# Sparse feed-forward: inner columns ordered by place in the quad, h turned one tile later, masks and masked product on POOL

## The chip, the cores and the metric

The kernel runs on one core of a Trainium2 chip. The metric is the device time of one launch in microseconds, the median of three runs. Lower is better.

## What is computed

A stack of six layers works on 1024 tokens of width 256, held as float32: a mixture of experts, attention, the mixture of experts again, a sparse feed-forward, a state-space layer, and the sparse feed-forward again with the same weights. The change touches only the two sparse feed-forward layers:

```python
def _sparsify_2to4(h):
    B, S, I = h.shape
    g = h.reshape(B, S, I // 4, 4)
    a = jnp.abs(g)
    _, idx = jax.lax.top_k(a, 2)
    pos = jnp.arange(4)
    mask = (pos == idx[..., 0:1]) | (pos == idx[..., 1:2])
    return (g * mask.astype(g.dtype)).reshape(B, S, I)
...
h = silu(x @ w_gate) * (x @ w_up)          # x: normalized tokens, 256 wide; h: 1024 wide
x = x + 0.5 * (_sparsify_2to4(h) @ w_down)
```

Of every four neighbouring inner columns (a quad) the two of largest magnitude stay, the others become zero; of equal magnitudes the earlier one stays.

## The kernel before

Each layer is a block in which the five engines run their own instruction streams in program order and meet at semaphores. `sparse_ffn_layer` walks over 8 token tiles of 128 tokens. In the profile's names its tiles carry the prefix `ffn_`; the same code runs twice, `ffn0` before the state-space layer and `ffn1` at the end of the kernel.

Products that need full precision are done in three passes (`matmul3`, lines 58 to 64): each float32 operand is split into a rounded high part and the remainder, both of type fp32r, and hi·hi, hi·lo and lo·hi are summed in PSUM. ACT makes a high part by a cast, DVE or POOL the low part by a subtraction.

For a tile t the steps are:

- `normalize` (DVE, L1226) makes xn; `turn_x` (PE, L1371) transposes it; `x_high` (ACT, L1330) and `x_low` (DVE, L1231) split it.
- `ups` (PE) computes gate and up for one half c of the inner columns, 12 matmuls of 512 columns for each half; `silu` (ACT, L1349) and `product` (DVE, L1239) turn them into half c of h.
- `mag` (ACT, L1359) takes magnitudes of the whole h. `sparsify` (DVE) compares them (`ffn_c`, L1252 to L1255), adds the comparisons to `wins` and `losses` (L1258 to L1260) and to a `score` per place (L1262 to L1265), and at the end (L1269, four operations) multiplies each place of h in place by its mask, score against a bound.
- `turn_h` (PE, L1397) transposes h in 8 pieces, `turned_high` (ACT, L1337) and `turned_low` (DVE, L1244) split it, `down` (PE) does 24 matmuls of 256 columns and `add` (DVE, L1274) adds half of the result to the residual.

The inner columns lie in memory as in the model, so that the four members of a quad are neighbours and one place of all 256 quads is read with a step of four float32 values (16 bytes).

Nothing but the order written in each engine's `body` and the semaphores sets the order of the work. In the body of tile t PE does ups(t, 0), the gate of ups(t, 1), turn_h(t−1), the up of ups(t, 1), turn_x(t+1), down(t−1). DVE does product(t, 0), turned_low(t−1), product(t, 1), x_low(t+1), sparsify(t), add(t−1), normalize(t+2). ACT does silu(t, 0), turned_high(t−1), silu(t, 1), x_high(t+1), mag(t). Tiles 3 to 6 run in a hardware loop of two tiles. POOL only makes the low parts of gate and down weights (L1199) at the start of the layer; there the weights are loaded in five transfers (L1206), the first of which holds the first half of the gate columns.

Of the kernel before, what the change touches and what calls it, by code (L numbers as in the profile page):

```python
# [1127 lines left out]
def sparse_ffn_layer(nc, xres, stats, ident, w_gate, w_up, w_down, tag, is_last=False):  # L1128
# [3 lines left out]
    with ExitStack() as ctx:  # L1132
# [24 lines left out]
        score = sp.sb("score", [P, 4, QUAD], BF16)  # L1157
        hT_hi = sp.sb("hT_hi", [P, KF, P], F32R)
# [16 lines left out]
        h_turned, hT_hi_done, hT_lo_done = (sp.sem(n) for n in ("h_turned", "hT_hi_done", "hT_lo_done"))  # L1175
        out_done, added = sp.sem("out_done"), sp.sem("added")
        ctx.callback(sp.clear_sems)
        block = ctx.enter_context(nc.Block())

        def tiles(eng, body):  # L1180

            for t in range(3):
                body(t, t % 2)
            with eng.Fori(1, TT // 2 - 1) as i:
                for b in (1, 0):
                    body(2 * i + 2 - b, b)
            body(TT - 1, 1)

        def static(t):
            return isinstance(t, int)  # L1190

        def part(n, c):
            return slice(0, D) if n == "down" else slice(c * BANK, (c + 1) * BANK)

        def split_low(eng, ops, n, c):

            eng.wait_ge(w_hi_done, w_parts.index((n, c)) + 1)
            cols = part(n, c)
            ops.tensor_tensor(w_lo[n][:, :, cols], w_raw[n][:, :, cols], f32(w_hi[n][:, :, cols]),  # L1199
                              ALU.subtract).then_inc(w_lo_done[n], 1)  # L1200

        @block.sync
        def _(sync):
            for n, c in w_parts:
                src = w_src[n].rearrange("(k p) n -> p k n", p=P)
                sync.dma_start(w_raw[n][:, :, part(n, c)], src[:, :, part(n, c)]).then_inc(loaded[n, c], 16)  # L1206

        @block.gpsimd
        def _(pool):
            for n, c in w_parts:  # L1210
                if n != "up":
                    split_low(pool, nc.gpsimd, n, c)

        @block.vector
        def _(dve):
# [1229 lines left out]
```

## Time and profile before

| | us |
|---|---|
| median of 3 runs (1861.74 to 1868.43) | 1865.56 |
| the profiled execution | 1868.16 |
| its span | 1866.3 |
| PE busy | 1601.7 (86% of the span) |
| DVE busy | 1146.5 (61%) |
| ACT busy | 863.0 (46%) |
| POOL busy | 442.4 (24%) |

The two sparse feed-forward layers stand at 892 to 1011 us (`ffn0`) and 1738 to 1860 us (`ffn1`) of the span. The other 1625 us are the layers that the change leaves alone. In the forty slices of the page the granted TensorE clock (PEclk) is 0.9 to 0.6 of full speed around the two ends of each of these layers.

### The profile page before, as it was taken

The numbers are of one execution on the slowest core, as the hardware profiler recorded it, in microseconds if no ns is written. First come the engines' busy times: TensorE is split into PE (matmuls) and PEld (weight loads), VectorE is DVE, ScalarE is ACT, GpSimd is POOL, SyncE is SP. The second block draws the span as 40 slices with busy tenths as digits, with TensorE's granted clock in tenths as the row PEclk, the third lists the DMA queues.
The fourth block names the chain that finished last, engine by engine and source line by source line (L and its number), as shares of the span: only waits on it lengthen the run. The fifth ranks groups of instructions, "written<-read, shape, count | busy, mean of one in ns | idle before, by whom it ended". The sixth has DMA issues, their size and how long they took to land. (4 is left out here: it accounts for less than half of the span.)

```text
span 1866.3 us, 25258 instructions
## 1 busy us (share of the span) xinstructions
PE 1601.7 (86%) x8136; PEld 1143.5 (61%) x8136; DVE 1146.5 (61%) x2073; ACT 863.0 (46%) x1270; POOL 442.4 (24%) x358
## 2 busy tenths in 40 slices
PE   3998399999999994998586877899998999998686
PEld 3665344444444443665475765787887888877575
DVE  4121688887878844221696765666766766764686
ACT  1222326655656662221332766566656655663321
POOL 1344400000000001343100112534534344433100
PEclk9999669999999996999797998999999999998888
DMA  8322100000000007422201000100101000100200
GB/s 302 95 46 37 43 21 12 10 4 12 12 12 11 0 1 273 92 46 38 87 1 29 21 8 19 29 18 23 29 12 29 23 17 23 29 12 12 68 0 23
DMA packets 70343, 73.78 MB, mean 40 GB/s; under 512 B 8480, under 2 KB 56992, under 8 KB 70240
## 3 DMA queue, kind: packets, MB, share of 16 engines
q1 hardware_dynamic: 60864, 58.35, 10.3%
q0 software_dynamic: 9376, 14.16, 4.3%
q8 instruction: 51, 0.84, 0.2%
q14 instruction: 52, 0.43, 0.1%
HBM read 56.50 MB, written 11.80 MB: 37 GB/s over the span
## 5 line engine op out<-in xcount | busy, mean ns | idle before, releaser
L784 DVE TENSOR_REDUCE attn_max_halves<-attn_scores 128x1 f32<-128x512 f32 x470 | 302.5, 686 | 70.4 <-PE attn_scores L1008 63.7
L913 ACT ACTIVATE attn_probs<-attn_scoresT 128x1024 f32<-128x1024 f32 x256 | 253.3, 1025 | 172.3 <-PE attn_scoresT L1021 171.8
L1008 PE MATMUL attn_scores<-attn_k_picks,attn_qT_pass 128*128 128x512 f32 x470 | 197.7, 452 | 5.6 <-DVE attn_max_halves L784 3.4
L1008 PEld LDWEIGHTS attn_scores<-attn_k_picks,attn_qT_pass 128*128 128x128 f32 x470 | 81.9, 188 | 152.6 <-DVE attn_max_halves L784 146.3
L1021 PE MATMUL attn_scoresT<-attn_qT_pass,attn_k_picks 128*128 128x512 f32 x512 | 169.0, 405 | 1.0 <-DVE attn_max_halves L784 1.0
L1447 DVE SCALAR_TENSOR_TENSOR ssm_scan_x<-ssm_scan_proj,ssm_w_conv,ssm_scan_x 128x1023 f32<-128x1023 f32 (+2 forms) x96 | 122.9, 1280 | 61.2 <-ACT ssm_scan_x L1442 58.2
L401 DVE TENSOR_TENSOR moe_h<-moe_silu,moe_up 128x512 f32<-128x512 f32 x46 | 31.6, 687 | 189.5 <-PE moe_up L516 189.5
L1035 PE MATMUL attn_o<-attn_probs,attn_v_group 128*32 128x512 f32 x1024 | 137.2, 608 | 0.6 <-ACT attn_probs L913 0.6
L2275 PE MATMUL ssm_scan_out<-ssm_scan_w_out,ssm_scan_v 128*128 128x256 f32 x464 | 118.2, 404 | 2.7 <-issue 2.7
L448 ACT ACTIVATE moe_silu<-moe_gate 128x512 f32<-128x512 f32 x46 | 27.5, 598 | 200.4 <-PE moe_gate L516 200.4
L62 PE MATMUL ssm_scan_proj<-ssm_xnT_hi,ssm_w_in_hi 128*128 128x512 f32 x256 | 115.1, 450 | 5.4 <-POOL ssm_scan_mask L1925 5.1
L286 POOL DMA_INDIRECT moe_sums<-moe_y,moe_token x46 | 73.0, 1588 | 165.2 <-DVE moe_y L410 159.2
L2142 ACT ACTIVATE ssm_scan_decay<-ssm_scan_cum,ssm_neg_cum 128x128 f32<-128x128 f32 x256 | 73.3, 368 | 79.0 <-PE ssm_scan_cum L2212 79.0
L1021 PEld LDWEIGHTS attn_scoresT<-attn_qT_pass,attn_k_picks 128*128 128x128 f32 x512 | 94.1, 189 | 22.3 <-ACT attn_probs L913 4.4
L63 PE MATMUL ssm_scan_proj<-ssm_xnT_lo,ssm_w_in_hi 128*128 128x512 f32 x256 | 105.9, 414 | 0.0
L64 PE MATMUL ssm_scan_proj<-ssm_xnT_hi,ssm_w_in_lo 128*128 128x512 f32 x256 | 105.6, 413 | 0.0
L2275 PEld LDWEIGHTS ssm_scan_out<-ssm_scan_w_out,ssm_scan_v 128*128 128x128 f32 x464 | 94.5, 205 | 17.5 <-issue 2.9
L1929 POOL TENSOR_TENSOR ssm_w_in_lo<-ssm_w_in,ssm_w_in_hi 128x512 fp32r<-128x512 f32 x31 | 42.2, 1362 | 239.8 <-ACT ssm_w_in_hi L2106 239.8
L516 PE MATMUL moe_gate<-moe_w_gate_up,moe_xT 128*128 x184 | 90.3, 614 | 1.3 <-ACT moe_xT L442 1.3
L2031 DVE SCALAR_TENSOR_TENSOR ssm_scan_x<-ssm_scan_x,ssm_d_skip,ssm_scan_y 128x1024 f32<-128x1024 f32 x32 | 41.0, 1281 | 80.9 <-PE ssm_scan_y L2253 80.9
L546 PE MATMUL moe_out<-moe_w_down,moe_hT 128*128 x368 | 87.1, 380 | 1.5 <-ACT moe_hT L454 1.5
L546 PEld LDWEIGHTS moe_out<-moe_w_down,moe_hT 128*128 128x128 f32 x368 | 69.8, 190 | 30.2 <-issue 23.0
(339 smaller groups left out, 3422.6 us busy)
## 6 DMA issues: line engine op xcount, KB each, us to landing
moe_w_gate_up<-in_moe_w SPq DMA_DIRECT2D x16, 512.0 KB, 11.2
moe_w_up<-in_moe_w SPq DMA_DIRECT2D x16, 512.0 KB, 11.1
moe_w_down<-in_moe_w SPq DMA_DIRECT2D x16, 512.0 KB, 11.0
ssm_w_in<-in_in_w SPq DMA_DIRECT2D x64, 128.0 KB, 2.2
attn_k_picks<-attn_kT SPq DMA_DIRECT2D x32, 128.0 KB, 2.4
ssm_scan_w_out<-in_out_w SPq DMA_DIRECT2D x8, 512.0 KB, 3.9
moe_sums<-main_residual SPq DMA_DIRECT2D x2, 1024.0 KB, 5.7
moe_rows<-moe_xn POOLq DMA_DIRECT2D x2, 1024.0 KB, 10.0
```

The source lines that it names most:

```text
L62: nc.tensor.matmul(out, lhs_hi, rhs_hi, start=start, stop=False)
L63: nc.tensor.matmul(out, lhs_hi, rhs_lo, start=False, stop=False)
L64: return nc.tensor.matmul(out, lhs_lo, rhs_hi, start=False, stop=stop)
L516: last = nc.tensor.matmul(bank[:].unsqueeze(1), xT[i % 2][:, k, :], w_in[name][:, bass.ds(e * KD + k, 1), :], start=(k == 0), stop=(k == K ...
L546: last = nc.tensor.matmul(out_ps[i % 2][:, 0:D].unsqueeze(1), hT[i % 2][:, k, :], w_dn[:, bass.ds(e * KI + k, 1), :], start=(k == 0), stop ...
L784: return nc.vector.tensor_reduce(rmax2[:, t, j, c:c + 1], chunk_bank(g, n), AX_X, ALU.max).then_inc(reduced, 1)
L913: nc.scalar.activation(probs[s % 2][:, 2 * pair:2 * pair + 2, :], st_ps[pair][:], ACT.Exp, scale=SCALE).then_inc(exp_done, 1)
L1008: nc.tensor.matmul(chunk_bank(g, n), qm[b][:, t * P:(t + 1) * P], kz[b][:, j, c * BANK:(c + 1) * BANK], start=True, stop=True).then_inc(sc ...
L1021: last = nc.tensor.matmul(st_ps[pair][:, j % 2, :], kz[b][:, j, kt * P:(kt + 1) * P], qe[b][:, half * BANK:(half + 1) * BANK], start=True, ...
L1035: last = nc.tensor.matmul(o_ps[j * STACK:(j + 1) * STACK, :], vg[b][:, kt, :], probs[s % 2][:, j, :], start=(kt == 0), stop=(kt == KT_TILE ...
L1447: return nc.vector.scalar_tensor_tensor(out[:, shift:], ps[:, :S - shift], w(k), out[:, shift:], ALU.mult, ALU.add)
L2275: last = nc.tensor.matmul(out[:, m, :], v[:, v_row(b * NORM_HEADS + jn), cols], w_out[:, jn, :], start=(jn == 0), stop=(jn == NORM_HEADS - 1))
```

## The change

The four places of a quad get blocks of their own: gate and up weights are reordered when they are split, so that h and its magnitudes are laid out as [place, quad] with 256 contiguous values for each place. The rows of the down weights are loaded in the matching order by four transfers. The four masks and the product of h with them move from DVE to POOL. PE, ACT and DVE run one tile further apart: `turn_h(t-1)` comes at the end of tile t, `down(t-2)` in the middle of it, and DVE does `sparsify(t-1)` at the start of tile t. The hardware loop is gone; the eight tiles are written out. The gate and up weights are loaded by rows (two transfers each) rather than by halves of the columns.

```diff
+        mask = sp.sb("mask", [P, 4, QUAD])
...
             eng.wait_ge(w_hi_done, w_parts.index((n, c)) + 1)
-            ops.tensor_tensor(w_lo[n][:, :, cols], w_raw[n][:, :, cols], f32(w_hi[n][:, :, cols]),
-                              ALU.subtract).then_inc(w_lo_done[n], 1)
+            for k in range(KD):
+                last = ops.tensor_tensor(in_places(w_lo[n], c)[:, k], by_place(w_raw[n], c)[:, k],
+                                         f32(in_places(w_hi[n], c)[:, k]), ALU.subtract)
+            last.then_inc(w_lo_done[n], 1)
...
+            for n in ("gate", "up"):
+                for k in range(KD):
+                    sync.dma_start(w_raw[n][:, k, :], src[n][k * P:(k + 1) * P, :]).then_inc(loaded[n, k], 16)
...
+            for t in range(TT):                                   # POOL
+                pool.wait_ge(scored, t + 1)
+                if t:
+                    pool.wait_ge(sparse, t)
+                for w, (op, bound) in enumerate(((ALU.is_ge, 2.0), (ALU.is_ge, 1.0), (ALU.is_le, 0.0), (ALU.is_le, 1.0))):
+                    last = nc.gpsimd.tensor_scalar(mask[:, w], score[:, w], bound, None, op)
+                last.then_inc(masked, 1)
+                pool.wait_ge(masked, t + 1)
+                nc.gpsimd.tensor_tensor(h[t % 2][:], h[t % 2][:], mask[:], ALU.mult).then_inc(sparse, 1)
...
-            def body(t, b):                                       # DVE
-                product(t, b, 0)
-                if not first:
-                    turned_low(t - 1)
-                product(t, b, 1)
-                if not last:
-                    x_low(t + 1, 1 - b)
-                sparsify(t, b)
-                if not first:
-                    add(t - 1)
+            for t in range(TT):
+                if t:
+                    sparsify(t - 1)
+                product(t, 0)
+                if t < LAST:
+                    x_low(t + 1)
+                if t >= 2:
+                    turned_low(t - 2)
+                    add(t - 2)
+                if t + 2 < TT:
+                    normalize(t + 2)
+                product(t, 1)
+            sparsify(LAST)
+            turned_low(LAST - 1)
+            add(LAST - 1)
+            if not is_last:
+                dve.wait_ge(added, LAST)
+                token_stats(nc, stats, xres, range(LAST))
+            turned_low(LAST)
+            add(LAST)
...
+            x_high(0)                                             # ACT
+            for n, c in w_parts:
+                split(n, c)
+            for t in range(TT):
+                silu(t, 0)
+                if t == 0:
+                    act.wait_ge(down_loaded, 64)
+                    nc.scalar.copy(w_dn_hi[:], w_dn[:]).then_inc(w_dn_hi_done, 1)
+                if t < LAST:
+                    x_high(t + 1)
+                silu(t, 1)
...
+                nc.scalar.activation(mag[:], h[t % 2][:], ACT.Abs).then_inc(mag_done, 1)
+                if t:
+                    turned(t - 1)
...
+            for t in range(TT):                                   # PE
+                ups(t, 0)
+                if t < LAST:
+                    turn_x(t + 1)
+                if t >= 2:
+                    down(t - 2)
+                ups(t, 1)
+                if t:
+                    turn_h(t - 1)
+            down(LAST - 1)
+            turn_h(LAST)
+            down(LAST)
```

`down` waits for the low parts of h in two halves of four pieces each, where it waited for both before its first matmul.

This is DVE's stream in one tile of the steady part before, from the last score of a tile to the last product of the next (`ffn_h<-ffn_silu,ffn_up` is `product`, `ffn_hT_lo` `turned_low`, `main_residual` `add`, `ffn_xT_lo` `x_low`):

```order
L1265 TENSOR_TENSOR ffn_score<-ffn_losses,ffn_c_23 128x256
L1269 SCALAR_TENSOR_TENSOR ffn_h<-ffn_score,ffn_h 128x256 x4
L1274 SCALAR_TENSOR_TENSOR main_residual<-ffn_out,main_residual 128x256
L1226 TENSOR_SCALAR ffn_xn<-main_residual,ffn_mean_var,ffn_rstd 128x256
L1239 TENSOR_TENSOR ffn_h<-ffn_silu,ffn_up 128x512
L1244 TENSOR_TENSOR ffn_hT_lo<-ffn_hT,ffn_hT_hi 128x512 x2
L1239 TENSOR_TENSOR ffn_h<-ffn_silu,ffn_up 128x512
L1231 TENSOR_TENSOR ffn_xT_lo<-ffn_xT,ffn_xT_hi 128x256
L1252 TENSOR_TENSOR ffn_c_13<-ffn_magnitude 128x512
```

And this is the same stretch of DVE's stream in the changed kernel:

```order
L1274 TENSOR_TENSOR ffn_score<-ffn_losses,ffn_c_23 128x256
L1252 TENSOR_TENSOR ffn_h<-ffn_silu,ffn_up 128x512
L1244 TENSOR_TENSOR ffn_xT_lo<-ffn_xT,ffn_xT_hi 128x256
L1279 TENSOR_TENSOR ffn_hT_lo<-ffn_hT,ffn_hT_hi 128x512 x2
L1284 SCALAR_TENSOR_TENSOR main_residual<-ffn_out,main_residual 128x256
L1239 TENSOR_SCALAR ffn_xn<-main_residual,ffn_mean_var,ffn_rstd 128x256
L1252 TENSOR_TENSOR ffn_h<-ffn_silu,ffn_up 128x512
L1259 TENSOR_TENSOR ffn_c_13<-ffn_magnitude 128x512
```

The four operations on h are gone, and `add` and `normalize` have moved between the two products of a tile.

On PE, before, the transposes of h stand inside the second half of `ups`, and `down` (`ffn_out`) follows at its end:

```order
L64 MATMUL ffn_gate<-ffn_w_gate_hi,ffn_xT_lo 128x512
L1397 MATMUL ffn_hT<-main_ident,ffn_h 128x128 x8
L62 MATMUL ffn_up<-ffn_w_up_hi,ffn_xT_hi 128x512
L63 MATMUL ffn_up<-ffn_w_up_lo,ffn_xT_hi 128x512
L64 MATMUL ffn_up<-ffn_w_up_hi,ffn_xT_lo 128x512
L62 MATMUL ffn_up<-ffn_w_up_hi,ffn_xT_hi 128x512
L63 MATMUL ffn_up<-ffn_w_up_lo,ffn_xT_hi 128x512
L64 MATMUL ffn_up<-ffn_w_up_hi,ffn_xT_lo 128x512
L1371 MATMUL ffn_xT<-main_ident,ffn_xn 128x128 x2
L62 MATMUL ffn_out<-ffn_w_down_hi,ffn_hT_hi 128x256
```

In the changed kernel `down` stands between the first half of `ups` (above it) and the second (below it), and the transposes of h close the tile:

```order
L64 MATMUL ffn_up<-ffn_w_up_hi,ffn_xT_lo 128x512
L1372 MATMUL ffn_xT<-main_ident,ffn_xn 128x128 x2
L62 MATMUL ffn_out<-ffn_w_down_hi,ffn_hT_hi 128x256
...
L64 MATMUL ffn_out<-ffn_w_down_hi,ffn_hT_lo 128x256
L62 MATMUL ffn_gate<-ffn_w_gate_hi,ffn_xT_hi 128x512
...
L64 MATMUL ffn_up<-ffn_w_up_hi,ffn_xT_lo 128x512
L1398 MATMUL ffn_hT<-main_ident,ffn_h 128x128 x8
```

So a `down` now stands ahead of the second half of gate and up in PE's queue, where it stood behind it.

## Rows read from the trace of the kernel before

**Rows 1.** Windows: stretch, length, busy time of each engine, granted clock, DMA

```profile
909.66:993.22 83.56, 68.70 (x381) 57.31 (x380) 73.79 (x152) 25.36 (x42) 1.33 (x1) 0.96 0.00 0
993.22:1010.87 17.65, 9.94 (x56) 9.13 (x56) 12.14 (x28) 2.23 (x3) 0.00 (x0) 0.71 0.00 0
1754.50:1842.46 87.96, 71.59 (x381) 60.11 (x380) 74.78 (x152) 25.54 (x42) 2.82 (x1) 0.92 0.00 1
1842.46:1860.42 17.96, 10.23 (x56) 9.42 (x56) 9.86 (x21) 2.23 (x3) 0.00 (x0) 0.71 0.00 1
```

**Rows 2.** Timeline of DVE in one tile of ffn1: start, duration, engine, line

```profile
1829.58 1.29 DVE L1244 TENSOR_TENSOR ffn_hT_lo<-ffn_hT,ffn_hT_hi 128x512 fp32r<-128x512 f32 x2
1830.85 0.69 DVE L1239 TENSOR_TENSOR ffn_h<-ffn_silu,ffn_up 128x512 f32<-128x512 f32 x1
1831.46 0.42 DVE L1231 TENSOR_TENSOR ffn_xT_lo<-ffn_xT,ffn_xT_hi 128x256 fp32r<-128x256 f32 x1
1832.67 1.10 DVE L1252 TENSOR_TENSOR ffn_c<-ffn_magnitude 128x512 bf16<-128x512 f32 x1 [0.79 <-ACT ffn_magnitude L1359]
...
1835.84 0.42 DVE L1258 TENSOR_TENSOR ffn_wins<-ffn_c,ffn_c 128x512 bf16<-128x512 bf16 x1
...
1837.63 2.19 DVE L1269 SCALAR_TENSOR_TENSOR ffn_h<-ffn_score,ffn_h 128x256 f32<-128x256 bf16 x4
```

**Rows 3.** Timeline of PE in the same tile

```profile
1830.92 0.39 PE L62 MATMUL ffn_out<-ffn_w_down_hi,ffn_hT_hi 128*128 128x256 f32 x1
...
1833.90 0.40 PE L62 MATMUL ffn_gate<-ffn_w_gate_hi,ffn_xT_hi 128*128 128x512 f32 x1
...
1836.65 0.39 PE L62 MATMUL ffn_gate<-ffn_w_gate_hi,ffn_xT_hi 128*128 128x512 f32 x1
...
1839.87 1.09 PE L1397 MATMUL ffn_hT<-main_ident,ffn_h 128*128 128x128 f32 x8 [1.70 <-DVE ffn_h L1269]
...
1841.96 0.40 PE L64 MATMUL ffn_up<-ffn_w_up_hi,ffn_xT_lo 128*128 128x512 f32 x1
```

**Rows 4.** Timeline in attention: a DVE sum of two SBUF operands, POOL idle, then busy

```profile
213.62 0.49 DVE L779 TENSOR_TENSOR attn_roped<-attn_qk_cos,attn_qk_sin 128x320 f32<-128x320 f32 x1
...
214.93 0.73 POOL L737 TENSOR_TENSOR attn_q_stack<-attn_roped,attn_q_stack 128x256 f32<-128x256 f32 x1
215.01 0.99 DVE L779 TENSOR_TENSOR attn_roped<-attn_qk_cos,attn_qk_sin 128x320 f32<-128x320 f32 x1
```

**Rows 5.** Groups by shape on POOL: count, busy time, mean ns, idle before

```profile
L1959 POOL TENSOR_TENSOR ssm_scan_squares<-ssm_scan_squares,ssm_scan_gate 128x1024 f32<-128x1024 f32 x24 | 56.8, 2367 | 8.9 <-ACT ssm_scan_gate L2150 8.9
...
L737 POOL TENSOR_TENSOR attn_q_stack<-attn_roped,attn_q_stack 128x256 f32<-128x256 f32 x8 | 5.9, 732 | 1.1
...
L745 POOL COPY attn_v_group<-attn_v_all 128x256 f32 x6 | 2.4, 402 | 188.4 <-PE attn_o L1035 188.4
```

**Rows 6.** Timeline of PE: restarts after idle time, and where the slow matmuls end

```profile
918.64 1.97 PE L1397 MATMUL ffn_hT<-main_ident,ffn_h 128*128 128x128 f32 x8 [3.50 <-DVE ffn_h L1269]
...
924.03 0.34 PE L62 MATMUL ffn_out<-ffn_w_down_hi,ffn_hT_hi 128*128 128x256 f32 x1
...
1777.29 1.84 PE L1397 MATMUL ffn_hT<-main_ident,ffn_h 128*128 128x128 f32 x8 [1.94 <-DVE ffn_h L1269]
...
1780.64 0.51 PE L63 MATMUL ffn_up<-ffn_w_up_lo,ffn_xT_hi 128*128 128x512 f32 x1
```

**Rows 7.** Timeline of ACT at the start of ffn1

```profile
1747.17 1.04 ACT L1320 CAST ffn_w_up_hi<-ffn_w_up 128x1024 fp32r<-128x1024 f32 x1 [0.33 <-DMA ffn_w_up<-in_ffn_up]
1748.23 1.28 ACT L1349 ACT_TABLE_LOAD   x1
1750.26 0.60 ACT L1349 ACTIVATE ffn_silu<-ffn_gate 128x512 f32<-128x512 f32 x1 [0.75 <-PE ffn_gate L64]
1750.76 1.90 ACT L1320 CAST ffn_w_down_hi<-ffn_w_down 128x2048 fp32r<-128x2048 f32 x1
```

**Rows 8.** Timeline of DVE at the end of ffn0

```profile
1005.44 2.38 DVE L75 BATCH_NORM_STATS2 main_token_stats<-main_residual 128x6 f32<-128x256 f32 x7
```

More of the change, by code:

```diff
@@ L1289, in _ @@
-            normalize(0, 0)
-            normalize(1, 1)
+                nc.vector.scalar_tensor_tensor(xres[:, t, :], out_ps[:], 0.5, xres[:, t, :], ALU.mult, ALU.add).then_inc(added, 1)
+            normalize(0)
+            normalize(1)
+            x_low(0)
             split_low(dve, nc.vector, "up", 0)
-            x_low(0, 0)
             split_low(dve, nc.vector, "up", 1)
-            for t in range(3):
-                body(t, t % 2)
-                normalize(t + 2, t % 2)
-            with dve.Fori(1, TT // 2 - 2) as i:
-                for b in (1, 0):
-                    body(2 * i + 2 - b, b)
-                    normalize(2 * i + 4 - b, b)
@@ L1318, in split @@
             def split(n, c):
-                act.wait_ge(loaded[n, c], 16)
-                nc.scalar.copy(w_hi[n][:, :, part(n, c)], w_raw[n][:, :, part(n, c)]).then_inc(w_hi_done, 1)
+                if c == 0:
+                    for k in range(KD):
+                        act.wait_ge(loaded[n, k], 16)
+                for k in range(KD):
+                    last = nc.scalar.copy(in_places(w_hi[n], c)[:, k], by_place(w_raw[n], c)[:, k])
+                last.then_inc(w_hi_done, 1)
             act.wait_ge(mv_done, TT)
@@ L1372, in turn_x, with ups @@
                 last.then_inc(x_turned, 1)
-            def ups(t, b, c, between=lambda: None):
+            def ups(t, c):
+                b = t % 2
                 pe.wait_ge(x_lo_done, t + 1)
-                if not (static(t) and t == 0):
+                if t:
                     pe.wait_ge(silu_done, 2 * t - 1 + c)
@@ L1406, in down @@
                 for k in range(KF):
[L1407 to L1408 removed]
+                    if k % 4 == 0:
+                        pe.wait_ge(hT_lo_done, 2 * t + k // 4 + 1)
+                    last = matmul3(nc, out_ps[:], (hT_hi[:, k, :], hT_lo[:, k, :]), (w_dn_hi[:, k, :], w_dn_lo[:, k, :]),
+                                   start=(k == 0), stop=(k == KF - 1))
                 last.then_inc(out_done, 1)
[L1411 to L1423 removed]
+            turn_x(0)
+            for t in range(TT):
+                ups(t, 0)
+                if t < LAST:
+                    turn_x(t + 1)
+                if t >= 2:
+                    down(t - 2)
+                ups(t, 1)
+                if t:
+                    turn_h(t - 1)
+            down(LAST - 1)
+            turn_h(LAST)
+            down(LAST)
 HM = 32
```

202 lines of the change are left out of this document (76 added, 126 removed).

## The prediction

> **What bounds the kernel now.** I first look for the stretches that the change can touch: two layers of some 120 us, and in each the distance between the second products of tile 0 and tile 7, read with the windows [rows 1]: 83.56 us in ffn0 and 87.96 us in ffn1, seven tiles each, so 11.9 and 12.6 us a tile. In neither is an engine full: DVE is busy for 73.79 of 83.56 us, PE for 68.70. So a chain that passes through several engines sets the pace, and I read the timelines of DVE and PE of one tile to find it [rows 2, 3]. From product(t, 1) at 1830.85 the magnitudes on ACT take until the first compare at 1832.67 (1.82 us); compares, sums and scores until the masked product at 1837.63 (4.96); the four masked products 2.19; then PE transposes h at 1839.87, ACT and DVE split it, and the next product starts at 1842.46. The round is 11.61 us. PE stands idle in it for 1.70 us, waiting for h. The reader is to see that only this round matters: work that is moved off DVE helps only as far as nothing else enters the round.
>
> **The compares.** Before, the four compares take 1832.67 to 1835.84, 3.17 us for 1536 results [rows 2]. They read float32 with a step of 16 bytes. A sum of 320 float32 values from two contiguous SBUF operands takes 0.49 us while POOL is idle [rows 4], about 1.0 ns a value beyond a fixed part, where the compares take 2.0. Contiguous, I put 512 results at what a product of 512 shows from start to start, 0.61 us, and 256 at what x_low shows when something follows it, some 0.34: with 0.11 for the wait behind the last, 0.61 + 0.34 + 0.34 + 0.72 = 2.01 us. That is 1.16 less; the bounds are 0 (the step was not the reason) and 2 (as fast as the bf16 operations, 0.42 for 512). So sparsify takes 3.80 us up to its last score. The masked products leave DVE (2.19).
>
> **The new round.** I follow the new order. DVE: sparsify(t−1), product(t, 0), x_low, turned_low(t−2), add(t−2), normalize, product(t, 1). PE: down(t−2), then ups(t, 1). product(t, 1) needs ups(t, 1), which stands behind down(t−2); that needs turned_low(t−2), which stands behind sparsify(t−1) on DVE, though its data have long been there; and sparsify(t−1) needs the magnitudes of product(t−1, 1). This closes in one tile: magnitudes 1.82, sparsify 3.80, product 0.61, x_low about 0.33, first half of turned_low 0.65 and 0.1 for the signal [rows 2], down 2.98 (1830.92 to 1833.90), ups(t, 1) until its product 3.02 (twelve matmuls take 2.75 from 1833.90 to 1836.65; less 0.23 for the last, and with 0.5 from that one's start to the product, 1841.96 to 1842.46) [rows 3]. Sum 13.31 us at full clock, against 11.61 before. What left the round is 2.19 + 1.16 us of DVE and the turning of h (2.6 us, 1839.87 to 1842.46); what entered it is down and half of ups, 6 us of PE that used to run beside sparsify.
>
> **PE idles longer.** After ups(t, 1) PE does the transposes (about 0.9), ups(t+1, 0) 2.75 and turn_x 0.35, and is then 4.0 us behind the start of product(t, 1), while down can start only at 1.82 + 3.80 + 0.61 + 0.33 + 0.75 = 7.31. That is 3.3 us idle in each tile. Before, 1.70 us idle left the clock at 2.4 GHz (eight transposes in 1.09 us [rows 3]); after 1.94 and 3.50 us idle they took 1.84 and 1.97, the level of 1.2 GHz, and matmuls stayed slow for 3.35 us (1777.29 to 1780.64) and 5.4 us (918.64 to 924.03) [rows 6]. Five restarts behind 1.93 us or more are of this kind, and four of them are slow for 3.0 to 3.6 us. Half of a slow stretch is lost: 1.7 us a tile by the four, 2.7 by the fifth, 0 if the clock holds. All of it falls on down and ups, on the round. I take 1.7.
>
> **POOL.** Four masks of 256 and a product of 1024. The product is a row, 2.37 us; a mask lies between a copy of 256, 0.40, and a two-operand operation of 256, 0.73 [rows 5]; it has one input, so I take 0.42, and with signals 4.2 us in all (5.5 with the upper end). From the last score to the moment PE wants the transposes there are 0.61 + 0.33 + 0.75 + 2.98 + 3.02 = 7.7 us. It is hidden in the steady part by 3.5 us, and the next compares come only after that. It shows at the two ends.
>
> In the trace a DVE operation with two SBUF operands goes from 0.49 to 0.99 us when POOL runs beside it [rows 4]. The Trainium skill (GPSIMD Engine Reference, Key points) says that POOL shares its SBUF interfaces with VectorE and contends with instructions that have two SBUF inputs. The trace agrees. By it the compares would lose what the layout gives them, 1.16 us a tile, if POOL's masks lay beside them; by the times above they meet only in tile 1, and there off the path.
>
> **First tiles.** From the start of product(0, 1) to that of product(1, 1): 1.82 + 3.80 + 0.61 + 0.33 + 0.33 = 6.9. Masks of tile 0 end at 1.82 + 3.80 + 4.2 = 9.8; transposes 0.85; ups(2, 0) and its product at 13.7; then 0.61 + 0.33 + 0.75 + 2.98 + 3.02: product(2, 1) starts at 21.4. Five rounds of 13.3 lead to tile 7: 87.9 us, before the loss by the clock.
>
> **End of the layer.** Before, 17.96 us in ffn1 and 17.65 in ffn0 [rows 1]. Now: 1.82 + 3.80 + 0.75 = 6.4 until down(6); 2.98, and 1.7 for the clock; turn_h(7), for which the masks are ready at 9.8, starts at 11.05 and gives down(7) 2.0 later (the 2.6 above less the second half); 2.98 + 0.3 + 0.42 gives 16.75. In ffn0 token statistics of 2.38 us [rows 8] now stand between add(6) and turned_low(7) on DVE and delay it by some 1.8.
>
> **Start of the layer.** The first split needed the first transfer alone; up now needs the fourth, landed at 1747.17. From there ACT does three more pairs of casts (3 × 1.04), a table load 1.28, silu 0.5, the down cast 1.9, x_high 0.4, silu 0.6 [rows 7]: product(0, 1) at 1755.0 instead of 1754.5. The casts read with a step of 16 bytes; nothing in the trace shows that on ACT. If they doubled like the compares, it is 3.1 more. I take 1.5 a layer, between 0.5 and 3.7, near the lower end since a cast reads one operand where the compare reads two.
>
 By that the casts double, and the sum below would be some 4 us higher.
>
> **Sum**, against the profiled 1868.16 us: ffn0 87.9 + 18.55 = 106.45 against 101.21 (+5.2); ffn1 87.9 + 16.75 = 104.65 against 105.92 (−1.3); starts +3.0; the clock, 6 tiles a layer, 12 × 1.7 = +20.4. Together +27.3. The profiled execution lies 2.6 us above the median; against the median of 1865.56 the forecast is 1893 us. Its own range, with 1.0 to 2.7 for the clock, 1 to 7.4 for the starts: +17 to +44.
>
> **Rivals.**
> - The clock holds at 2.4 GHz. For it: DVE's period is regular and PE is busy for 9.7 us in 13.3. Against: all five longer idle times were followed by 1.2 GHz. Price: 12 × 1.7 less, +7, 1872 us. Chance 0.12.
> - The layout does not speed up the compares. For it: no row here shows the same operation contiguous. 16 × 1.16 = 19 more, 1911 us. Chance 0.09.
> - POOL sets the pace. For it: a mask reads bf16 and writes float32, which no POOL row shows. From 1.3 us a mask on POOL exceeds the 7.7 us. At 1.5 a round is 1.0 longer (10 rounds), and the ends 4.3 and 2 longer in each layer: +23, 1916 us. Chance 0.10.
> - Faster than before: DVE's part of the round shrinks further. If the compares ran at the rate of the bf16 operations (0.8 us less, 16 times, −13), PE's idle time fell to 2.5 us and the clock stayed up as well, 3.9 + 3.0 − 13 = −6, 1860 us. It is faster from compares below 1.2 us in all with the clock at full. Against: the contiguous float32 sum [rows 4] has no such rate. Chance 0.09.
>
> The forecast has 0.60. About 0.3% (5.6 us) is what a measurement of this kernel can tell from no change. Faster takes the last rival, 0.09; within 0.3% a part of the clock's rival and of low ends together, 0.10; slower the rest, 0.81. The range of 8 in 10 goes from the clock's rival to the two dear ones: 1870 to 1915 us.
>
> **What would show it.** In the profile after: PE's longest idle time in a tile before the first `ffn_out`, 3.3 us, released by DVE `ffn_hT_lo`; tiles at a distance of 13.3 to 16 us; matmuls of `ffn_out` at 0.21 us from start to start; compares at 0.6 and 0.34; POOL 4.2 us a tile and not waited for in the steady part. The prediction is wrong if PE does not wait for `ffn_hT_lo`, if the tiles stand closer than 12 us, or if POOL's product releases the transposes in every tile.

## The result

The changed kernel takes 1911.95 us (median of 4 runs, 1909.73 to 1917.06), against 1865.36 us for the kernel before (1861.74 to 1868.43) on the same chip: a ratio of 1.025, 95% interval [1.023, 1.028], so 46.6 us slower. The forecast was 1893 us, +27.3: the sign and the mechanism of the tiles held, the size was two fifths too small. The profiled execution took 1912.81 us, with a span of 1911.0 against 1866.3.

I cut each layer at four marks on DVE: the reciprocal of the deviations, product(0, 1), product(7, 1), and the end of the last add.

| stretch (us) | ffn0 before | after | ffn1 before | after | both | forecast |
|---|---|---|---|---|---|---|
| start, to product(0, 1) | 15.74 | 21.54 | 15.01 | 21.21 | +12.0 | +3.0 |
| product(0, 1) to product(7, 1) | 83.56 | 100.81 | 87.96 | 100.74 | +30.0 | +24.7 |
| from there to the end | 17.65 | 18.35 | 17.96 | 17.18 | −0.1 | −0.3 |

Together +41.9 us; the forecast's middle row holds its 20.4 for the clock. The other 2.8 us of the span lie outside the two layers, 2.2 of them ahead of ffn0, where nothing was changed. In the profiled executions of the runs below the time ahead of ffn0 differs by up to 7 us, so a layer's own windows tell more than the whole time where only a few us are in question.

### The profile page after: what moved, and what is told of

The parts are those of the page before. It is cut to its first block and busy times, and to the rows that moved or that the text cites. A ratio compares the mean times of both kernels' runs of the same rounds, so it can differ in the third digit from the quotient of the medians.

```text
span 1911.0 us, 25244 instructions
## 1 busy us (share of the span) xinstructions
PE 1614.2 (84%) x8136; PEld 1159.6 (61%) x8136; DVE 1109.6 (58%) x2013; ACT 869.2 (45%) x1278; POOL 535.9 (28%) x442
## 5 line engine op out<-in xcount | busy, mean ns | idle before, releaser
L2277 PE MATMUL ssm_scan_out<-ssm_scan_w_out,ssm_scan_v 128*128 128x256 f32 x464 | 114.2, 394 | 2.7 <-issue 2.7
L2277 PEld LDWEIGHTS ssm_scan_out<-ssm_scan_w_out,ssm_scan_v 128*128 128x128 f32 x464 | 91.6, 199 | 16.3 <-issue 2.9
L62 PE MATMUL ffn_out<-ffn_w_down_hi,ffn_hT_hi 128*128 128x256 f32 x128 | 48.0, 375 | 52.7 <-DVE ffn_hT_lo L1279 52.7
L1222 POOL TENSOR_SCALAR ffn_mask<-ffn_score 128x256 f32<-128x256 bf16 x64 | 52.8, 851 | 132.0 <-DVE ffn_score L1274 132.0
```

Of the source, the lines that this page charges most:

```text
L62: nc.tensor.matmul(out, lhs_hi, rhs_hi, start=start, stop=False)
L2277: last = nc.tensor.matmul(out[:, m, :], v[:, v_row(b * NORM_HEADS + jn), cols], w_out[:, jn, :], start=(jn == 0), stop=(jn == NORM_HEADS - 1))
```

## The profile after

The windows of the two layers of the changed kernel, to be laid beside [rows 1] (length, busy time of PE, weight loads, DVE, ACT and POOL, granted clock, DMA):

```profile
917.63:1018.44 100.81, 73.36 (x363) 64.08 (x364) 50.51 (x122) 23.26 (x39) 39.95 (x35) 0.85 0.00 1
1018.44:1036.79 18.35, 9.82 (x63) 9.00 (x61) 9.99 (x25) 3.09 (x5) 5.67 (x5) 0.81 0.00 0
1787.29:1888.03 100.74, 73.31 (x363) 64.05 (x364) 50.48 (x121) 23.25 (x39) 39.92 (x35) 0.83 0.00 1
1888.03:1905.21 17.18, 10.12 (x64) 9.37 (x61) 7.71 (x18) 3.09 (x5) 5.67 (x5) 0.80 0.00 1
```

From product(0, 1) to product(7, 1) DVE is busy for 50.5 us where it was 73.8 in ffn0 and 74.8 in ffn1: it was relieved, as the change meant it to be. This stretch still grew, by 17.3 us in ffn0 and 12.8 in ffn1, and the granted clock fell from 0.96 and 0.92 to 0.85 and 0.83. DVE has less to do, and the time is set by a longer chain of waits.

The timeline of DVE for one round of ffn1, from product(4, 1) to product(5, 1), answers to [rows 2]:

```profile
1842.02 0.69 DVE L1252 TENSOR_TENSOR ffn_h<-ffn_silu,ffn_up 128x512 f32<-128x512 f32 x1 [2.08 <-PE ffn_up L64]
1843.84 0.69 DVE L1259 TENSOR_TENSOR ffn_c<-ffn_magnitude 128x512 bf16<-128x512 f32 x1 [1.13 <-ACT ffn_magnitude L1360]
1844.45 0.42 DVE L1260 TENSOR_TENSOR ffn_c<-ffn_magnitude 128x256 bf16<-128x256 f32 x1
...
1845.84 0.42 DVE L1265 TENSOR_TENSOR ffn_wins<-ffn_c,ffn_c 128x512 bf16<-128x512 bf16 x1
...
1847.52 0.68 DVE L1252 TENSOR_TENSOR ffn_h<-ffn_silu,ffn_up 128x512 f32<-128x512 f32 x1
1848.11 0.41 DVE L1244 TENSOR_TENSOR ffn_xT_lo<-ffn_xT,ffn_xT_hi 128x256 fp32r<-128x256 f32 x1
1848.45 1.28 DVE L1279 TENSOR_TENSOR ffn_hT_lo<-ffn_hT,ffn_hT_hi 128x512 fp32r<-128x512 f32 x2
1854.77 0.42 DVE L1284 SCALAR_TENSOR_TENSOR main_residual<-ffn_out,main_residual 128x256 f32<-128x256 f32 x1 [5.05 <-PE ffn_out L64]
...
1857.68 0.69 DVE L1252 TENSOR_TENSOR ffn_h<-ffn_silu,ffn_up 128x512 f32<-128x512 f32 x1 [2.16 <-PE ffn_up L64]
```

The reader is to see the compares in 2.00 us (1843.84 to 1845.84), where they took 3.17, and then DVE waiting 5.05 us for down. PE in the same round:

```profile
1845.36 0.38 PE L1372 MATMUL ffn_xT<-main_ident,ffn_xn 128*128 128x128 f32 x2
1849.27 0.55 PE L62 MATMUL ffn_out<-ffn_w_down_hi,ffn_hT_hi 128*128 128x256 f32 x1 [3.53 <-DVE ffn_hT_lo L1279]
...
1854.32 0.41 PE L64 MATMUL ffn_out<-ffn_w_down_hi,ffn_hT_lo 128*128 128x256 f32 x1
1854.53 0.52 PE L62 MATMUL ffn_gate<-ffn_w_gate_hi,ffn_xT_hi 128*128 128x512 f32 x1
```

PE waits 3.53 us for `ffn_hT_lo`, and then down takes 5.26 us (1849.27 to 1854.53) instead of 2.98: its matmuls start 0.213 us apart where they were 0.12. The round is 1.82 + 3.68 + 0.59 + 0.34 + 0.82 + 5.26 + 3.15 = 15.66 us, and each term is one that the forecast names; only down is much longer, by the clock. Rounds of 14.4 to 14.7 us and of 15.6 to 16.0 mostly take turns, 15.1 in the mean of ten. In the round behind this one, one of the shorter, down takes 4.4 us (1864.93 to 1869.37): the matmuls of its last third start 0.12 us apart again.

The start of ffn1, DVE, then POOL, then ACT:

```profile
1782.85 0.42 DVE L1244 TENSOR_TENSOR ffn_xT_lo<-ffn_xT,ffn_xT_hi 128x256 fp32r<-128x256 f32 x1 [0.22 <-ACT ffn_xT_hi L1331]
1783.19 4.17 DVE L1239 TENSOR_SCALAR ffn_xn<-main_residual,ffn_mean_var,ffn_rstd 128x256 f32<-128x256 f32 x1
1787.29 0.68 DVE L1252 TENSOR_TENSOR ffn_h<-ffn_silu,ffn_up 128x512 f32<-128x512 f32 x1
```

```profile
1776.80 3.35 POOL L1197 TENSOR_TENSOR ffn_w_gate_lo<-ffn_w_gate,ffn_w_gate_hi 128x512 fp32r<-128x512 f32 x2 [1.68 <-ACT ffn_w_gate_hi L1322]
1782.63 4.59 POOL L1216 TENSOR_TENSOR ffn_w_down_lo<-ffn_w_down,ffn_w_down_hi 128x2048 fp32r<-128x2048 f32 x1 [2.48 <-ACT ffn_w_down_hi L1353]
```

```profile
1769.97 2.08 ACT L1322 CAST ffn_w_gate_hi<-ffn_w_gate 128x512 fp32r<-128x512 f32 x2 [2.08 <-DMA ffn_w_gate<-in_ffn_gate]
1772.55 2.12 ACT L1322 CAST ffn_w_up_hi<-ffn_w_up 128x512 fp32r<-128x512 f32 x2 [0.51 <-DMA ffn_w_up<-in_ffn_up]
```

The casts take 2.08 us for 1024 values where they took 1.04 [rows 7]; here they read with the step of 16 bytes. And the normalization of tile 2, normally 0.41 us, lasts 4.17: it starts 0.56 us behind POOL's `ffn_w_down_lo` and ends 0.14 us behind it. product(0, 1) stands right behind it.

## Experiments

All times are medians; changed means 1911.95 us. Unless said otherwise an experiment starts from the changed kernel.

**early_normalize.** The normalization of tile 2 in another place.

```diff
             x_low(0)
+            normalize(2)
...
-                if t + 2 < TT:
+                if t and t + 2 < TT:
                     normalize(t + 2)
                 product(t, 1)
```

> The changed kernel with one move: the normalization of tile 2 stands right behind x_low(0) on DVE, and no longer in front of product(0, 1), where it took 4.2 us in both layers while POOL computed w_down_lo. Theory A (the normalization, SBUF to SBUF, is held by POOL's work on two SBUF operands; the product, which reads PSUM, is not): it takes 0.41 us at its new place and product(0, 1) starts 3.7 to 4.0 us sooner in each layer: 7 to 8 us less than the changed kernel, 1904 us. Theory B (whatever stands there on DVE is held until POOL ends): product(0, 1) takes the 4 us itself, no change, 1912 us.

1906.5 us (1905.7 to 1907.9), 5.4 less. product(0, 1) came 17.05 and 17.62 us behind the reciprocal, 4.5 and 3.6 sooner: theory A for the product. But from there to product(1, 1) it took 8.4 and 8.5 us instead of 7.0 and 6.9, so 8.1 us are gained and 3.0 given back. The timeline of DVE and of POOL in ffn1 shows who is held now:

```profile
1779.62 0.69 DVE L1252 TENSOR_TENSOR ffn_h<-ffn_silu,ffn_up 128x512 f32<-128x512 f32 x1 [0.49 <-PE ffn_up L64]
1781.43 2.21 DVE L1259 TENSOR_TENSOR ffn_c<-ffn_magnitude 128x512 bf16<-128x512 f32 x1 [1.13 <-ACT ffn_magnitude L1361]
1783.56 0.41 DVE L1260 TENSOR_TENSOR ffn_c<-ffn_magnitude 128x256 bf16<-128x256 f32 x1
```

```profile
1778.47 4.61 POOL L1216 TENSOR_TENSOR ffn_w_down_lo<-ffn_w_down,ffn_w_down_hi 128x2048 fp32r<-128x2048 f32 x1 [2.56 <-ACT ffn_w_down_hi L1354]
```

The product, which reads PSUM, passes beside POOL in 0.69 us; the first compare, with two SBUF operands, waits until POOL's operation ends. Part of the gain was handed on to the next operation that POOL holds.

**warm_clock.** Filling PE's wait with matmuls that count for nothing.

```diff
             pe.wait_ge(added, t)
+        if t < LAST - 1:
+            for _ in range(20):
+                nc.tensor.matmul(out_ps[:], w_hi["gate"][:, 0, 0:P], w_hi["gate"][:, 0, 0:D], start=True, stop=True)
```

> The changed kernel with 20 extra matmuls of 256 columns (about 2.5 us at full clock) on PE, in the 3.5 us that it waits before down in tiles 0 to 5; they write the accumulator of down, which down then overwrites, so no result changes. Theory A (the idle time lets the clock fall, and the fall costs 1.8 us a tile, the measured 15.1 us less the 13.3 us worked out at full clock): tiles stand 13.3 to 13.5 us apart, down takes 3.0 us in each, 12 x 1.8 = 21 us less than the changed kernel, 1890 us. Theory B (the clock is low for another reason, or its loss is made up by slack elsewhere): tiles stay at 15 us, 1912 us or more. If the clock is low when they start they last 4.2 us and delay down by 0.7 us a tile, 1920 us.

1888.5 us (1885.9 to 1890.5), 23.5 less: theory A. Between their marks the two layers of the profiled execution are 19 us shorter; most of the rest lies ahead of ffn0 (5.4 us), where nothing differs. Its windows from product(1, 0) to product(7, 1):

```profile
917.38:1003.30 85.92, 74.58 (x469) 66.81 (x470) 47.79 (x110) 20.89 (x35) 40.13 (x35) 0.94 0.00 1
1777.20:1863.28 86.08, 74.77 (x469) 66.96 (x470) 47.77 (x110) 20.90 (x35) 40.12 (x35) 0.94 0.00 1
```

Inside, the rounds from tile 2 to tile 6 are 13.15 us long and the last 12.8, with down at full clock. Only the wait was filled, with work that is thrown away, and the kernel became faster: so the clock's share was 9.3 us a layer (100.8 and 100.7 us from product(0, 1) to product(7, 1) against 91.4 and 91.6), and what is left, 13.15, is the round itself.

**product_first.** Opening the round at ups(t, 1).

```diff
-                if t >= 2:
-                    down(t - 2)
                 ups(t, 1)
+                if t >= 2:
+                    down(t - 2)
...
+                product(t, 1)
                 if t >= 2:
                     turned_low(t - 2)
                     add(t - 2)
                 if t + 2 < TT:
                     normalize(t + 2)
-                product(t, 1)
```

> The changed kernel with two swaps: on PE ups(t, 1) stands ahead of down(t-2), and on DVE product(t, 1) ahead of turned_low(t-2), add(t-2) and the normalization. Theory A (what makes the changed kernel slow is that down and ups(t, 1) close the round from product to product; the masks on POOL cost nothing): the round loses 5.3 us of down and 3.0 of ups and is then set by PE or DVE at 9.8 to 10.5 us a tile: 12 x 4.8 = 58 us less than the changed kernel, 1854 us. Theory B (POOL, now 5.8 us a tile, and the normalization that it holds up set the pace once the round is open): 12 to 12.5 us a tile, 1876 to 1882 us. Theory C (the round was not the reason): no change, 1912 us.

1866.7 us (1861.6 to 1871.6), 45 less and level with the kernel before. Rounds are 11.27 us, between theory A (at most 10.5) and B (12 and more). The stretch from product(0, 1) to product(7, 1) is 22.6 and 22.8 us shorter. The starts are 4.3 and 3.5 shorter as well, since product(0, 1) now stands ahead of the held normalization, and the ends 4.8 and 3.1 longer. What A missed stands in the timelines of DVE and PE:

```profile
1800.09 0.69 DVE L1252 TENSOR_TENSOR ffn_h<-ffn_silu,ffn_up 128x512 f32<-128x512 f32 x1 [1.35 <-PE ffn_up L64]
1800.69 1.28 DVE L1279 TENSOR_TENSOR ffn_hT_lo<-ffn_hT,ffn_hT_hi 128x512 fp32r<-128x512 f32 x2
```

```profile
1801.53 0.36 PE L62 MATMUL ffn_out<-ffn_w_down_hi,ffn_hT_hi 128*128 128x256 f32 x1 [1.54 <-DVE ffn_hT_lo L1279]
```

turned_low now stands behind product(t, 1), which waits for ups(t, 1), and PE in turn waits 1.54 us for turned_low: PE's 9.7 us of work plus this exchange is the round. PE does not wait for POOL in it.

**early_low.** Opening the round at turned_low.

```diff
-                    sparsify(t - 1)
+                    sparsify(t - 1, lambda: turned_low(t - 2) if t >= 2 else None)  # called behind the compares
...
                 if t >= 2:
-                    turned_low(t - 2)
                     add(t - 2)
```

> The changed kernel with one move on DVE: turned_low(t-2) stands between the compares and the sums of sparsify(t-1), no longer behind product(t, 0) and x_low. Nothing moves on PE, ACT or POOL. Theory A (down was late only because turned_low stood behind sparsify, and the clock only fell because PE waited for it): down starts 1.82 + 2.0 + 0.65 us after the product, PE waits under 1 us and stays at 2.4 GHz, the round is 1.82 + 2.0 + 0.75 + 2.98 + 3.02 = 10.6 us: 12 x 4.5 = 54 us less than the changed kernel, 1858 us. Theory B (POOL, 5.8 us a tile, then releases the transposes late and sets the pace, 12 us a tile or more): 1875 us or more. Theory C (the clock stays low): 12.3 us a tile, 1878 us.

1878.7 us (1878.4 to 1879.8), 33 less. The time is the one that theory C gave (1878), but not by its rounds of 12.3 us: every other round is 10.50 us, as theory A has it, and the ones between are 13.5. There PE waits for POOL, as in theory B, and the clock is low afterwards:

```profile
943.05 0.35 PE L62 MATMUL ffn_out<-ffn_w_down_hi,ffn_hT_hi 128*128 128x256 f32 x1 [0.81 <-DVE ffn_hT_lo L1280]
951.07 1.29 PE L1397 MATMUL ffn_hT<-main_ident,ffn_h 128*128 128x128 f32 x8 [2.17 <-POOL ffn_h L1225]
```

One place on DVE, nothing else moved, is worth 33 of the 46.6 us: most of what made the changed kernel slow is that turned_low stands behind sparsify. With turned_low early POOL's part is no longer hidden, and the kernel is still 13 us slower than before.

**pool_longer.** One more product of 1024 values on POOL in each tile.

```diff
                 last.then_inc(masked, 1)
+                nc.gpsimd.tensor_tensor(spare[:], w_dn[:, 0:4, :]..., w_dn[:, 4:8, :]..., ALU.mult)
```

> The changed kernel with one more operation on POOL in each tile, a product of 1024 values into a spare tile between the masks and the masked product, 2.4 us. Theory A (POOL is hidden in the steady part, with 3.9 us between its end and the transposes, and shows at tile 2 and at the end): rounds stay at 15.1 us, at most 2.4 us more at each of the two places of a layer: 5 to 10 us more than the changed kernel, 1917 to 1922 us. Theory B (POOL sets the pace): 2.4 us in each tile, 16 x 2.4 = 38 us more, 1950 us.

1922.8 us (1920.2 to 1924.8), 10.9 more, where POOL was given 38 us of work: theory A, at the upper end of its range. The rounds behind tile 2 are unchanged (14.2 to 15.8); product(1, 1) to product(2, 1) took 2.1 and 2.9 us more, the ends 3.4 and 4.1. That most of these are over the 2.4 can be the clock, lower behind the longer waits; it was not measured apart.

**masks_on_dve.** POOL's part undone, all else as changed.

```diff
+                for w, (op, bound) in enumerate(...):
+                    last = nc.vector.scalar_tensor_tensor(hq[:, w], score[:, w], bound, hq[:, w], op, ALU.mult)
+                last.then_inc(sparse, 1)
...
-                    last = nc.gpsimd.tensor_scalar(mask[:, w], score[:, w], bound, None, op)
-                nc.gpsimd.tensor_tensor(h[t % 2][:], h[t % 2][:], mask[:], ALU.mult).then_inc(sparse, 1)
```

> The changed kernel with the four masked products back on DVE (1.43 us and a signal of 0.1, on columns by place), everything else as changed: what POOL's part is worth. Theory A (DVE's work up to turned_low is in the round, POOL's is not): each of 12 steady rounds takes 1.5 us more or a little above it for the longer idle time of PE, +18; the transposes of tile 0 and of the last tile come up to 4.3 us sooner and the compare of tile 1 is not held (2.1), -10 to -13: 1917 to 1921 us. Theory B (POOL's part is what makes the changed kernel slow): 1890 us or less.

1930.8 us (1926.6 to 1935.2), 18.8 more and beyond theory A's 1921. Rounds are 17.1 us: 1.5 for the masked products, 0.5 for the clock, since PE now waits 5.00 us ahead of every down and all of them run at the lower clock. The relief at tile 2 was 1.1 and 1.3 us and not 4; at the ends there was none (1.1 and 0.6 us more), since down(6) starts later. So the masks on POOL are the good part of the order, 19 us.

**layout_alone.** Columns by place with the order of work of before. The loads by rows, the written-out tiles and the two halves in which down waits stay as changed.

```diff
+                product(t, 0)
+                if t:
+                    turned_low(t - 1)
+                product(t, 1)
+                if t < LAST:
+                    x_low(t + 1)
+                sparsify(t)          # with the masked products, on DVE
+                if t:
+                    add(t - 1)
```

> One part of the change alone: columns ordered by place in the quad, with the loads and casts that go with it, but the order of work, the masked products on DVE and the place of down as before. Theory A (contiguous compares save 1.28 us of the 11.61 us round, 4.96 to 3.68, and nothing replaces them): tiles stand 10.3 to 10.5 us apart, 14 x 1.28 = 18 us less than before, 2 less at the ends, and 2 to 6 us more at each start for the casts that read with a step of 16 bytes: 1849 to 1857 us. Theory B (PE, busy for 9.8 us a tile, or another wait takes the place of the compares): tiles stay above 11.2 us, the starts remain, 1868 to 1876 us.

1835.1 us (1831.6 to 1839.5), a ratio to before of 0.985 [0.983, 0.987] and 29 us less, and better than theory A. The masked products of the four places and the windows of both layers:

```profile
1746.67 1.43 DVE L1267 SCALAR_TENSOR_TENSOR ffn_h<-ffn_score,ffn_h 128x256 f32<-128x256 bf16 x4
```

```profile
911.33:979.11 67.78, 65.14 (x384) 55.44 (x384) 60.05 (x152) 25.26 (x42) 1.43 (x1) 1.00 0.00 1
979.11:994.27 15.16, 9.39 (x56) 8.61 (x54) 10.15 (x28) 2.15 (x3) 0.00 (x0) 0.77 0.00 0
1741.07:1808.85 67.78, 65.14 (x384) 55.45 (x384) 60.05 (x153) 25.27 (x42) 1.69 (x1) 1.00 0.00 1
```

I had priced the compares alone; the masked products also fell, from 2.19 [rows 2] to 1.43 us, 10.6 us in 14 rounds. The rest comes from rounds that were longer than 11.6 before: 13.6 us behind product(0, 1) in ffn0, 13.8, 13.2, 13.3 and 12.7 at the start of ffn1, with PE at a lower clock in them; here all are 9.68. So the two stretches are 15.8 and 20.2 us shorter and the ends 2.5 and 2.8, while the starts are 3.6 and 5.3 longer. PE is busy for 65.14 of 67.78 us and the clock is granted in full. PE has become the bound. That the written-out tiles have a part in this was not tested apart; in ffn0 before, rounds in the hardware loop (11.6 to 11.7 us) are as long as those outside it behind tile 1.

**strided_on_pe.** The layout alone, but the ordering left to PE's reads.

```diff
-                    last = nc.scalar.copy(in_places(w_hi[n], c)[:, k], by_place(w_raw[n], c)[:, k])
+                    last = nc.scalar.copy(w_hi[n][:, k], w_raw[n][:, k])
...
-                                       (w_hi[n][:, k, cols], w_lo[n][:, k, cols]), start=(k == 0), stop=(k == KD - 1))
+                                       (by_place(w_hi[n], c)[:, k], by_place(w_lo[n], c)[:, k]), start=(k == 0), stop=(k == KD - 1))
```

> The layout alone (work in the order of before), with the weights kept as they come: casts and low parts read and write them contiguously, in rows of 1024, and PE reads its moving operand with a step of 16 bytes. Theory A (PE takes a moving operand with a step of 16 bytes as fast as a contiguous one): ups stay at 2.75 us for twelve matmuls, tiles at 9.7 us, and product(0, 1) comes 3 to 5 us sooner in each layer, since the casts cost 1.04 and not 2.1 for 1024 values: 1825 to 1829 us against 1835. Theory B (PE pays for the step as the casts do, twice as long): ups take 5.5 us each, PE needs 15.2 us a tile, 16 x 5.5 = 88 us more, 1915 us or above.

1912.3 us (1909.4 to 1917.8), 77 more than the layout alone: theory B, a little below its 1915. At a granted clock of 1.00 three ups matmuls in a row read:

```profile
963.94 0.64 PE L64 MATMUL ffn_gate<-ffn_w_gate_hi,ffn_xT_lo 128*128 128x512 f32 x1
964.40 0.65 PE L62 MATMUL ffn_gate<-ffn_w_gate_hi,ffn_xT_hi 128*128 128x512 f32 x1
964.86 0.65 PE L63 MATMUL ffn_gate<-ffn_w_gate_lo,ffn_xT_hi 128*128 128x512 f32 x1
```

They start 0.46 us apart, where a contiguous operand gives 0.23, and tiles stand 15.04 us apart. Of the two, casting with the step once, at the start, is the cheap way.

**layout_x_low_first, layout_warm_start, down_low_in_pieces.** Three tries at the start of the layout alone, each on top of the last.

```diff
+            x_low(0)
             split_low(dve, nc.vector, "up", 0)
-            x_low(0)
```

> The layout alone (work in the order of before, masked products on DVE), with x_low(0) on DVE ahead of the low part of up, which waits for a cast. Theory A (PE's first matmul at 1732.74 waited for x_low(0), which stood behind that low part; the low part of gate was ready at 1730.1): PE starts 2.5 us sooner in each layer, product(0, 1) 2 us sooner, the tiles stay at 9.68 us: 4 us less than the layout alone, 1831 us. Theory B (the low parts of the second half, 1735.7 on POOL and 1737.6 on DVE, hold ups(0, 1) anyway): 0 to 1 us less, 1834 us.

1835.8 us (1832.1 to 1843.5), no change. product(0, 1) did come 2.6 and 2.3 us sooner, but product(0, 1) to (7, 1) took 70.7 instead of 67.8 us: in ffn0 the first compare met POOL's `ffn_w_down_lo` and lasted 2.35 us, until 0.55 us behind its end. PE then waited 3.29 us for the masked product, and its clock fell (0.53 granted from 924 to 927 us): product(1, 1) came 12.2 us behind product(0, 1), not 9.7.

```diff
             turn_x(0)
+            for _ in range(32):
+                nc.tensor.transpose(hT_ps[0][:, 0, :], ident, ident)
```

> The kernel layout_x_low_first with 32 extra transposes of the identity on PE behind turn_x(0), in its wait of 8 us and more for the weights. Theory A (the first twelve matmuls run at 0.43 us from start to start, the lower clock, and it is on the path): at the full clock ups(0, 0) takes 2.75 and not 5.1 us, 1 to 2 us less in each layer, 1828 us. Theory B (the low parts of the second half end last): same time as without them, 1831 us. If the transposes outlast the wait: up to 2 us more, 1834 us.

1833.9 us (1828.6 to 1839.4), not told apart from the layout alone. The clock was up (ups(0, 0) at 0.23 us from start to start), product(0, 1) no sooner than without (16.77 against 16.72 us in ffn0): theory B, the low parts of the second half hold it.

```diff
-            nc.gpsimd.tensor_tensor(w_dn_lo[:], w_dn[:], f32(w_dn_hi[:]), ALU.subtract).then_inc(w_dn_lo_done, 1)
+            for k in range(KF):
+                last = nc.gpsimd.tensor_tensor(w_dn_lo[:, k], w_dn[:, k], f32(w_dn_hi[:, k]), ALU.subtract)
+            last.then_inc(w_dn_lo_done, 1)
```

> The kernel layout_warm_start with the low part of down on POOL in 8 operations of 256 values in place of one of 2048. What is told apart is how long POOL keeps DVE off: the first compare took 2.35 us instead of 0.69 in layout_x_low_first, until POOL's one operation ended. Theory A (DVE waits for the operation that POOL is in, and gets in between two): the compare takes at most 1.3 us, product(1, 1) comes 1 to 1.5 us sooner in each layer, 2 to 3 us less than layout_warm_start, 1831 us. Theory B (back-to-back operations of POOL keep DVE off as long as one long one): the compare still ends when the last piece does, no change, 1834 us.

1837.9 us (1835.8 to 1842.1), no gain. The compares of tile 0 in ffn0:

```profile
913.78 1.23 DVE L1252 TENSOR_TENSOR ffn_c<-ffn_magnitude 128x512 bf16<-128x512 f32 x1 [0.79 <-ACT ffn_magnitude L1358]
914.94 0.96 DVE L1253 TENSOR_TENSOR ffn_c<-ffn_magnitude 128x256 bf16<-128x256 f32 x1
915.82 0.95 DVE L1254 TENSOR_TENSOR ffn_c<-ffn_magnitude 128x256 bf16<-128x256 f32 x1
916.70 1.23 DVE L1255 TENSOR_TENSOR ffn_c<-ffn_magnitude 128x512 bf16<-128x512 f32 x1
```

```profile
910.96 6.41 POOL L1217 TENSOR_TENSOR ffn_w_down_lo<-ffn_w_down,ffn_w_down_hi 128x256 fp32r<-128x256 f32 x8 [2.69 <-ACT ffn_w_down_hi L1349]
```

Theory A holds for the mechanism (1.23 us, at most one piece waited for) and fails for the time: each compare now pays 0.54 us, four of them 2.2, and POOL takes 6.41 us instead of 4.58.

## Why the prediction was right in sign and short in size

The time of 1911.95 us lies in the stated 1870 to 1915, but that is in part luck. The sum's own range was +17 to +44, and +46.6 is above it. What carried the stated range up to 1915 were the two dear rivals, no gain by the layout and POOL setting the pace, and neither came true.

- **The round.** Right. At full clock it is 13.15 us (warm_clock) for a forecast of 13.31, made of the seven terms named. early_low, which takes sparsify's second half, product(t, 0) and x_low out of it (1.68 + 0.59 + 0.34 in the rows above), gives 10.50 in the rounds without a wait for POOL. Of the steps only one is moved, and the round follows.
- **The compares.** Right: 2.00 us against 2.01. With it the rival without a gain by the layout is out, and the one with compares below 1.2 us. The masked products' own gain from the layout (2.19 to 1.43) was not seen; in the changed kernel they are on POOL, so it costs the forecast nothing, but it is 10.6 of the some 18 us by which layout_alone beat its forecast.
- **PE's wait and the clock.** Right: 3.5 us released by DVE `ffn_hT_lo` for 3.3 forecast, and 2.0 us a round lost (15.1 in the mean, against 13.1 in the same rounds of warm_clock) for 1.7. The rival in which the clock holds is out: PE waits in every steady tile, and DVE's wait for down is 4.00 to 5.05 us there, against 2.69 at full clock.
- **POOL.** Hidden in the steady part, as said, but mis-sized. The rows:

```profile
L1222 POOL TENSOR_SCALAR ffn_mask<-ffn_score 128x256 f32<-128x256 bf16 x32 | 26.4, 851 | 66.0 <-DVE ffn_score L1274 66.0
L1225 POOL TENSOR_TENSOR ffn_h<-ffn_h,ffn_mask 128x1024 f32<-128x1024 f32 x8 | 19.2, 2401 | 0.7
```

A mask is 0.85 us where I took 0.42, beyond my upper end of 0.73: one input, but twice the copy of [rows 5]. The masks with the product take 5.8 us a tile and not 4.2. In the steady part there were still 4.0 us to spare (POOL ends at 1853.44, PE comes to the transposes at 1857.41), and pool_longer shows that it bears 2.4 more. The rival in which POOL sets the pace needed 1.3 us a mask and is out. It shows where I said it would, at tile 2, and there for more. The compares do meet it in tile 1, off the path as forecast: in ffn1 the one of 256 at 1796.63 lasts 2.56 us instead of 0.42, until 0.27 us behind the end of POOL's product, and DVE then waits 3.15 us for ACT anyway.
- **First tiles.** product(0, 1) to product(1, 1): 6.97 and 6.94 for 6.9. From there to product(2, 1): 18.23 and 18.58 for 16.2 (14.5 and 1.7 of clock). PE at tile 2 of ffn0:

```profile
929.34 1.97 PE L1398 MATMUL ffn_hT<-main_ident,ffn_h 128*128 128x128 f32 x8 [7.91 <-POOL ffn_h L1225]
```

POOL ends 6.1 us behind the last score instead of 4.2, about the missing 2.0 of ffn0 and most of the 2.4 of ffn1. The clock's loss falls here on the transposes and ups (1.97 us for the eight, 1.09 at full clock), not on down, and is of the size assumed.
- **The start is the step that failed**: +12.0 us for +3.0, where the bounds of the two layers together were 1 to 7.4. Of the 5.8 and 6.2 us, early_normalize takes 4.5 and 3.6 away, so that 1.3 and 2.6 are left for the doubled casts, the later first use and the slower low parts together. These lie inside the bounds of 0.5 to 3.7, and their sum of 3.9 is near the 3.0 that was put in. What had no term at all is that normalize(2) now stands in front of product(0, 1) and beside POOL's `ffn_w_down_lo`. I had looked for POOL beside the compares and found them apart, and did not run down the list of the other SBUF-to-SBUF operations that the new order puts beside POOL. The order of DVE shows it, and the 4.59 us of that operation was in the trace before. The Trainium skill (SBUF — State Buffer, Who interferes with whom) says that DVE in a mode with two ports, or with two SBUF inputs, and POOL keep each other out for a whole instruction, whoever comes first. The trace agrees where POOL came first: 4.17 us for a normalization, which has one SBUF tensor as input, and I had weighed the rule for two inputs alone.
- **The casts.** They doubled, from 1.04 to 2.08 us, where I had kept my value near the lower end because a cast reads one operand. The rule of the Trainium skill on lines of 16 bytes (SBUF — State Buffer, Door 1: The DMA port swizzle), read as holding for ACT too, gave that; the page names no engine. The time did not follow: four casts cost 4.2 us a layer more, but only 1.3 and 2.6 us are left at the starts. Part of it can be hidden under the transfers; no run shows where it went.
- **The ends.** 18.35 and 17.18 for 18.55 and 16.75.

The sum: 9.0 us missing at the starts, 5.3 in the tiles (4.4 of it at tile 2), 0.2 at the ends, 2.8 outside the layers; the medians lie 1.9 us further apart than the spans.

The parts of the change, each on top of the last: the layout with its loads and written-out tiles −29 us (to 1835), the order of work +96 (masks_on_dve, 1931), the masks on POOL −19 (1912). The layout alone beats both kernels; none of the three tries at its start was faster by more than its runs scatter. Open is how much of the start is the casts alone, since no run took only them away, and whether the order of the change with turned_low early and ups(t, 1) ahead of down would also reach PE's 9.7 us a tile: it was not tried.

## What to carry to other kernels

Before moving work off a busy engine, close the loop of the new order on paper, instruction by instruction and engine by engine: here 3.3 us left DVE's part of it and 6 us of PE's entered. In this deeper pipeline it was worth 33 us to issue the late stage's last small step (turned_low) ahead of most of the next tile's long block. And list every operation that the new order puts beside a long POOL operation, with where its operands lie: here a normalization and a compare, which read and write SBUF alone, waited for POOL's end, and a product and x_low, which read PSUM, did not.

## What the runs showed that I had not expected

- A step of 16 bytes in float32 costs on every engine that was seen with it: ACT's cast doubles (1.04 to 2.08 us), PE's moving operand doubles (0.23 to 0.46 us a matmul of 512), DVE's compare takes 1.6 times as long (0.69 us for 512 results, 1.10 with the step), and POOL's low part goes from 2.34 to 3.0 us for 1024 values.
- Twenty matmuls that count for nothing, put into a wait of 3.5 us, make the kernel 23.5 us faster, 19 us of it in the two layers.
- A long POOL operation holds one DVE operation until it ends (4.17 us for 0.41); cut into eight it holds each a little and costs 1.8 us more itself.
